# The list loop of route: POOL makes the two products of the high digit's one-hot rows, and DVE compares the high digit first in a chunk

## The chip, the cores and the metric

The kernel runs on one core of one Trainium2 chip. The metric is the device time of one execution in microseconds, median over runs. It is one program of many phases, with a barrier of all engines between them.

## The reference, cut to what matters

The whole is a small vision network: patches are projected to rows of 192, a retention layer follows, then a mixture of experts (16 experts, each picks its 1030 best rows out of 8240 by score), an attention layer, a second mixture (8 experts, two for each row). The change lies in the routing of the first mixture:

```python
scores = jax.nn.sigmoid(x @ gate_weight.T)
topk_score, topk_ids = jax.lax.top_k(scores.T, capacity)      # 16 experts, capacity 1030 of 8240 rows
xg = x[topk_ids]
...
y = jnp.zeros((n, d), x.dtype).at[topk_ids.reshape(-1)].add(out.reshape(-1, d))
shared = jax.nn.silu(hidden_states @ Ws_g.T) * (hidden_states @ Ws_u.T) @ Ws_d.T
return y + shared
```

The order of the chosen rows within an expert's list does not matter to the result.

## The kernel before, in words

`phase_route` finds each expert's threshold by a search over the bits of the score, numbers the chosen rows, and turns these numbers into lists of row indices. The shared expert (`shared_up`, `shared_silu`, `shared_mult`, `shared_rows`, `shared_down`) is computed beside both, ten steps in the search and ten in the list loop.

The list loop has NC = 10 chunks of T = 103 rows (on partitions). In a chunk there are 128 columns (8 images by 16 experts). A chosen row has a place in its expert's list, split into a low digit (0 to 63, plus 1 so that 0 means not chosen) and a high digit (0 to 16). For each column the loop makes a one-hot row of the low digit (64 wide, `hot_lo`, bf16) and two scaled one-hot rows of the high digit (17 wide each, `hot_hi`): the first holds the number of the row's tile, the second the row's number within the tile. One small matmul a column, `hot_hi` transposed by `hot_lo`, adds tile and row number into the right place of the list in PSUM: 128 matmuls a chunk (L785). They are called the list matmuls here.

A chunk on each engine, before:

- PE (TensorE): `shared_up` (three slices of two times two float32 matmuls, L715), `shared_down` (12 matmuls, L725), then it waits for `hot_ready` and does the 128 list matmuls, which end with `hot_used`.
- ACT (ScalarE): the silu of each slice (L800).
- DVE (VectorE): `list_chunk`. It waits for `hot_used` of the chunk before the last (`hot_lo` and `hot_hi` have two halves), then four compares of the low digit (32 columns each, L928), with the three products of the shared expert (L825, which read PSUM) between them; then the compare of the high digit into `hit` (L933), the product of `hit` with `tile0` (L937) and with `row` (L939), which releases PE; the addition of 1 to `tile0` (L942), and the two additions of `shared_rows` (L834), which wait for `shared_down`.
- POOL (GpSimd): memsets at the start of the phase, then 20 DMAs of the scores to DRAM (L705), for which it waits until `turned_out` is 9, like PE and DVE ahead of the loop; after that only the wait for these DMAs.
- SP: loads `h_in` and stores `y_out` of the shared expert, by `y_ready`.

A shared slice uses one of two pairs of PSUM banks: PE's slice f waits for the shared product f - 1 of DVE, and `shared_down` for all three.

`hot_hi` lies in `wide`, and `hit` has one buffer. The order within an engine is that of the code; between engines semaphores alone count. `zero` is a buffer of zeros that PE uses to open and close the accumulation.

Of the kernel before, what the change touches and what calls it, by code (L numbers as in the profile page):

```python
# [8 lines left out]
BF16 = mybir.dt.bfloat16  # L9
I32 = mybir.dt.int32  # L10
U32 = mybir.dt.uint32
ALU = mybir.AluOpType
# [9 lines left out]
T = 103  # L22
NC = SEQ // T
# [17 lines left out]
LB = 64  # L41
HB2 = -(-CAP // LB)
# [3 lines left out]
def names(ctx, nc):  # L46

    sems = []

    def sb(name, shape, dt=F32):
        return ctx.enter_context(nc.sbuf_tensor(name, shape, dt))

    def sem(name):
        sems.append(nc.alloc_semaphore(name))
        return sems[-1]

    def clear():  # L60
        nc.clear_and_free_semaphores(sems)
        nc.all_engine_barrier()

    ctx.callback(clear)
    return sb, sem
# [538 lines left out]
def phase_route(nc, psum, inp, h1, xg, x1T, y, ids, ident, ident_in, consts, consts_in):  # L604
# [9 lines left out]
    FC = FS0 // 128  # L614
# [3 lines left out]
    with ExitStack() as ctx:  # L618
        sb, sem = names(ctx, nc)
        gate, same, before, consts32, row = (consts[n] for n in ("gate", "same", "before", "consts32", "row"))  # L620
        wg, wu, wd = (consts[n] for n in ("wg", "wu", "wd"))
        gpad = sb("rt_gpad", [DP, DC, B, 128])
        iota_lo = sb("rt_iota_lo", [T, LB], BF16)
        iota_hi = sb("rt_iota_hi", [T, HB2], BF16)
        tile0 = sb("rt_tile0", [T, 128], BF16)
# [16 lines left out]
        hot_lo = sb("rt_hot_lo", [T, 2, 128, LB], BF16)  # L642
        hit = sb("rt_hit", [T, 128, HB2], BF16)

        hot_hi = wide[0:T, :, :].rearrange("p k n -> p (k n)").bitcast(BF16)[:, 0:2 * 128 * 2 * HB2] \
            .rearrange("p (a n k) -> p a n k", a=2, n=128)
        zero = sb("rt_zero", [128, 512], BF16)
        idp = sb("rt_idp", [128, 512])
        idT = sb("rt_idT", [128, 4, 128])

# [5 lines left out]
        consts_ready = sem("rt_consts_ready")  # L656
# [4 lines left out]
        step = sem("rt_step")  # L661
        sums_full = sem("rt_sums_full")
        turned, turned_out = sem("rt_turned"), sem("rt_turned_out")
        hit_ready, hot_ready, hot_used = sem("rt_hit_ready"), sem("rt_hot_ready"), sem("rt_hot_used")
        ids_open, ids_full, idp_ready = sem("rt_ids_open"), sem("rt_ids_full"), sem("rt_idp_ready")
        idT_full, idT_ready, ids_ready = sem("rt_idT_full"), sem("rt_idT_ready"), sem("rt_ids_ready")
# [28 lines left out]
        @block.gpsimd  # L695
        def _(pool):
            pool.memset(gpad[:], 0.0).then_inc(zeroed, 1)
            pool.memset(ones, 1.0).then_inc(zeroed, 1)
            pool.memset(zero[:], 0.0).then_inc(zeroed, 1)

            pool.wait_ge(turned_out, 9)
            rows = xg.rearrange("(b c p) d -> p c b d", b=B, c=NC)
            for c in range(NC):
                for lanes in LANES:
                    pool.dma_start(rows[lanes, c, :, D:D + E0], scT[lanes, c, :].rearrange("p (b e) -> p b e", b=B)) \  # L705
                        .then_inc(scores_out, 16)
            pool.wait_ge(scores_out, 32 * NC)

        def shared_up(pe, j, slices=range(FC)):
# [20 lines left out]
        @block.tensor  # L730
        def _(pe):
            pe.wait_ge(ident_in, 16)
            pe.wait_ge(consts_in, ROUTE_CONSTS)
            pe.wait_ge(gpad_ready, 1)
            for s, n in enumerate((W4, W4, SEQ - 2 * W4)):
                for b in range(B):
                    for k in range(DC):
                        last = pe.matmul(psum[:, s, 0:n], gpad[:, k, b, :], x1T[:, k, b, s * W4:s * W4 + n],
                                         start=(b == 0 and k == 0), stop=(b == B - 1 and k == 1))
                last.then_inc(logits_full, 1)  # L740
            pe.wait_ge(score_ready, 3)
            with pe.Fori(0, LOOPS) as j:
                def total(s):
                    pe.wait_ge(counted, j * STEPS + (s + 1))

                    pe.wait_ge(keep_ready, j * STEPS + s)
                    pe.matmul(TOTAL, same[:], count[:], start=True, stop=True).then_inc(totalled, 1)
                shared_up(pe, j, (0,))
                total(0)
                shared_up(pe, j, (1,))  # L750
                total(1)
                shared_up(pe, j, (2,))
                shared_down(pe, j, (0,))
                total(2)
                shared_down(pe, j, (1,))

            def sums(n, weights, rhs, bank):
                pe.wait_ge(step, n)
                pe.matmul(psum[:, bank, 0:1], weights[:], rhs, start=True, stop=True).then_inc(sums_full, 1)

            sums(1, same, small[:, 0:1], 6)
            sums(3, before, rank[:, SEQ - 1:SEQ], 7)
            sums(7, before, rank[:, SEQ - 1:SEQ], 5)

            pe.wait_ge(step, 12)
            for n, src in enumerate((hi, lo, score)):
                for s, c0 in enumerate(range(0, NC, 4)):
                    if 3 * n + s >= 3:
                        pe.wait_ge(turned_out, 3 * n + s - 2)
                    for c in range(c0, min(c0 + 4, NC)):  # L770
                        last = pe.transpose(psum[0:T, s, (c - c0) * 128:(c - c0 + 1) * 128],
                                            src[:, c * T:(c + 1) * T], ident[:])
                    last.then_inc(turned, 1)
            pe.matmul(LISTS, zero[:, 0:128], zero[:], start=True, stop=False, skip_group_check=True)
            pe.wait_ge(turned_out, 9)
            with pe.Fori(0, NC // 2) as i:
                for half in range(2):
                    c = i * 2 + half
                    shared_up(pe, c + LOOPS)
                    shared_down(pe, c + LOOPS)  # L780
                    pe.wait_ge(hot_ready, c + 1)
                    for b in range(B):
                        for e in range(E0):
                            q, g = e % 2, e // 2
                            last = pe.matmul(psum[LB * q:LB * q + 2 * HB2, 6, g * LB:(g + 1) * LB],  # L785
                                             hot_hi[:, half, b * E0 + e, :], hot_lo[:, half, b * E0 + e, :],
                                             start=False, stop=False, skip_group_check=True)
                    last.then_inc(hot_used, 1)
            pe.matmul(LISTS, zero[:, 0:128], zero[:], start=False, stop=True, skip_group_check=True).then_inc(ids_full, 1)
            pe.wait_ge(idp_ready, 1)  # L790
            for g in range(4):
                last = pe.transpose(psum[:, 7, g * 128:(g + 1) * 128], idp[:, g * 128:(g + 1) * 128], ident[:])
            last.then_inc(idT_full, 1)
# [45 lines left out]
        def _(dve):  # L839
# [81 lines left out]
            def list_chunk(c, half, first):  # L921

                lo_c = loT[:, bass.ds(c, 1), :].rearrange("p c n -> p (c n)")
                hi_c = hiT[:, bass.ds(c, 1), :].rearrange("p c n -> p (c n)")
                if not first:
                    dve.wait_ge(hot_used, c - 1)
                for f in range(FC + 1):
                    dve.tensor_tensor(hot_lo[:, half, f * 32:(f + 1) * 32, :],  # L928
                                      lo_c[:, f * 32:(f + 1) * 32].unsqueeze(2).to_broadcast([T, 32, LB]),
                                      iota_lo[:].unsqueeze(1).to_broadcast([T, 32, LB]), ALU.is_equal)  # L930
                    if f < FC:
                        shared_mult(dve, c + LOOPS, (f,))
                dve.tensor_tensor(hit[:], hi_c.unsqueeze(2).to_broadcast([T, 128, HB2]),  # L933
                                  iota_hi[:].unsqueeze(1).to_broadcast([T, 128, HB2]), ALU.is_equal).then_inc(hit_ready, 1)
                dve.wait_ge(hit_ready, c * 2 + 1)

                dve.tensor_tensor(hot_hi[:, half, :, 0:HB2], hit[:], tile0[:].unsqueeze(2).to_broadcast([T, 128, HB2]),  # L937
                                  ALU.mult)
                dve.tensor_scalar(hot_hi[:, half, :, HB2:2 * HB2], hit[:], row[:, 0:1], None, ALU.mult) \  # L939
                    .then_inc(hot_ready, 1)  # L940
                dve.wait_ge(hot_ready, c + 1)
                dve.tensor_scalar(tile0[:], tile0[:], 1.0, None, ALU.add).then_inc(hit_ready, 1)  # L942
                shared_rows(dve, c + LOOPS)

            for half in range(2):
                list_chunk(half, half, True)
# [8 lines left out]
            for side in range(2):  # L955
                for odd in range(2):
                    for q in range(2):
# [3 lines left out]
                        first = LB * q + odd  # L961
# [2170 lines left out]
```

## Time and profile before

| | us |
|---|---|
| runs, median (lowest to highest of 3) | 4561.05 (4549.51 to 4570.84) |
| profiled execution, own time | 4569.56 |
| its span | 4567.8 |
| PE busy | 4034.8 (88%) |
| DVE busy | 2484.5 (54%) |
| ACT busy | 1438.0 (31%) |
| POOL busy | 1249.9 (27%) |

The span is cut by the page into 40 slices of 114 us. The list loop, from about 656 to 870 us, is in slices 6 to 8 (counted from 1):

```profile
PE   8899878699999997665999999999959969899996
DVE  1576468622222222876878787877814355444442
POOL 0221010144444443553010001001012110077775
PEclk9999988899999998775999999999975589999998
```

Each digit is a busy share in tenths (9 is 90% or more); PEclk is the clock that TensorE was granted, in tenths of full speed, where 1.0 is 2.4 GHz and 0.5 is 1.2 GHz. DVE has 6, 8 and 6 there, POOL 1, 0 and 1. The chain that the page follows back from the last instruction stays in the last phase and says nothing of this loop, so the views of single stretches are used below.

### The profile page before, as it was taken

To read this page: it belongs to the slowest core of one execution; us is meant where nothing else is said; L and a number is where in the kernel's file an instruction comes from. 1 tells how busy PE (TensorE), PEld (TensorE's weight loads), DVE (VectorE), ACT (ScalarE), POOL (GpSimd) and SP (SyncE) were. 2 spreads that over 40 slices of the span, in tenths; PEclk is the share of its full clock that TensorE was granted. 3 is DMA by queue.
4 is the path that set the end of the run, shared out by engine and by line. 5 is a ranking of instruction groups with operands and counts; after the bars stand their busy time and mean duration, and the time that the engine had idled before them with its cause. 6 is when DMAs were issued, how large, how long until landed. Compare 5 with 4: busy or idle time off the path is not lost. (4 is left out here: it accounts for less than half of the span.)

```text
span 4567.8 us, 74772 instructions
## 1 busy us (share of the span) xinstructions
PE 4034.8 (88%) x23898; PEld 2458.2 (54%) x23898; DVE 2484.5 (54%) x4593; ACT 1438.0 (31%) x2890; POOL 1249.9 (27%) x1415
## 2 busy tenths in 40 slices
PE   8899878699999997665999999999959969899996
PEld 7788555466666665331333333333315646677774
DVE  1576468622222222876878787877814355444442
ACT  0122110011111111341677777777741111111111
POOL 0221010144444443553010001001012110077775
PEclk9999988899999998775999999999975589999998
DMA  6222111322222221345342224223225211267776
GB/s 217 60 67 54 32 38 28 99 61 60 60 60 60 60 60 28 118 132 107 49 62 44 44 48 61 44 44 51 39 62 158 76 37 46 66 163 172 174 172 154
DMA packets 335914, 361.61 MB, mean 79 GB/s; under 512 B 50364, under 2 KB 297107, under 8 KB 334095
## 3 DMA queue, kind: packets, MB, share of 16 engines
q1 hardware_dynamic: 252191, 274.75, 24.4%
q0 software_dynamic: 61312, 63.66, 8.9%
q10 hardware_dynamic: 22256, 20.93, 1.6%
q8 instruction: 122, 2.00, 0.2%
q14 instruction: 33, 0.27, 0.0%
HBM read 247.51 MB, written 117.00 MB: 80 GB/s over the span
## 5 line engine op out<-in xcount | busy, mean ns | idle before, releaser
L2033 DVE TENSOR_REDUCE at_mx<-psum 128x1 f32<-128x998 f32 (+1 forms) x768 | 884.5, 1189 | 247.2 <-PE psum L1858 246.8
L1988 ACT ACTIVATE at_p<-psum 128x512 f32<-128x512 f32 (+3 forms) x1536 | 851.2, 588 | 294.2 <-PE psum L1932 264.3
L1932 PE MATMUL psum<-at_q,at_k 99*128 99x512 bf16 (+3 forms) x1536 | 518.9, 380 | 21.5 <-issue 16.5
L1858 PE MATMUL psum<-at_k,at_q 96*128 96x512 bf16 (+3 forms) x1536 | 472.9, 390 | 69.4 <-POOL at_identb L1815 31.9
L1918 PE MATMUL psum<-at_p,at_v 128*32 128x486 f32 (+3 forms) x3072 | 405.1, 600 | 1.0 <-ACT at_p L1988 0.7
L1932 PEld LDWEIGHTS psum<-at_q,at_k 99*128 99x128 bf16 (+1 forms) x1536 | 155.0, 102 | 423.9 <-ACT at_p L1988 271.7
L1193 ACT ACTIVATE ex_silu<-psum 128x384 f32<-128x384 f32 (+1 forms) x288 | 131.5, 457 | 774.4 <-PE psum L1137 581.7
L1224 DVE TENSOR_TENSOR ex_hT<-ex_silu,psum 128x384 f32<-128x384 f32 (+1 forms) x288 | 147.5, 512 | 417.1 <-ACT ex_silu L1193 230.3
L1830 POOL DMA_DIRECT2D o_rows<-at_o x96 | 48.5, 505 | 1140.3 <-DVE at_mx L2033 967.0
L1159 PE MATMUL psum<-ex_wd,ex_hT 128*128 128x192 f32 (+1 forms) x1728 | 291.5, 327 | 0.0
L1858 PEld LDWEIGHTS psum<-at_k,at_q 96*128 96x128 bf16 (+1 forms) x1536 | 151.9, 105 | 230.6 <-DVE at_mx L2033 64.0
L1159 PEld LDWEIGHTS psum<-ex_wd,ex_hT 128*128 128x128 f32 (+1 forms) x1728 | 264.1, 179 | 15.9 <-issue 3.6
L2794 POOL DMA_INDIRECT h_rows<-mx_ys,mx_to x144 | 229.3, 1592 | 59.4 <-issue 59.4
L2948 DVE TENSOR_TENSOR mx_hT<-mx_silu,psum 128x256 f32<-128x256 f32 x216 | 91.0, 421 | 271.0 <-ACT mx_silu L2905 212.5
L2905 ACT ACTIVATE mx_silu<-psum 128x256 f32<-128x256 f32 x216 | 82.8, 383 | 479.1 <-PE psum L2847 424.0
L1085 POOL DMA_INDIRECT y_rows<-ex_ys,ex_to x144 | 223.4, 1551 | 33.5 <-issue 33.5
L1132 PE MATMUL psum<-ex_xT,ex_wg 128*128 128x384 f32 (+1 forms) x576 | 230.0, 481 | 0.0
L1133 PE MATMUL psum<-ex_xT,ex_wu 128*128 128x384 f32 (+1 forms) x576 | 213.3, 452 | 0.0
L1137 PE MATMUL psum<-ex_xT,ex_wr 64*128 64x384 f32 (+1 forms) x576 | 207.7, 476 | 0.8
L1138 PE MATMUL psum<-ex_xT,ex_wr 64*128 64x384 f32 (+1 forms) x576 | 207.7, 476 | 0.0
L2765 POOL TENSOR_TENSOR mx_pad<-ident 128x1 f32<-128x1 f32 x144 | 66.1, 459 | 353.6 <-DVE mx_idx L2914 301.9
L1050 POOL TENSOR_TENSOR ex_pad<-ident 128x1 f32<-128x1 f32 x127 | 41.5, 327 | 438.0 <-DVE ex_ys L1237 430.9
(361 smaller groups left out, 7030.7 us busy)
## 6 DMA issues: line engine op xcount, KB each, us to landing
mx_wd<-in_e_dT SPq DMA_DIRECT2D x72, 288.0 KB
qk_parts<-hd_parts SPq DMA_DIRECT2D x32, 579.4 KB, 3.8
at_k<-qk_parts SPq DMA_DIRECT2D x144, 128.8 KB, 5.0
at_q<-qk_parts SPq DMA_DIRECT2D x144, 124.8 KB, 4.6
tok_p<-in_x SPq DMA_DIRECT2D x12, 1176.0 KB
mx_wg<-in_e_gT SPq DMA_DIRECT2D x72, 192.0 KB
mx_wu<-in_e_uT SPq DMA_DIRECT2D x72, 192.0 KB
v_rows<-hd_v_out SPq DMA_DIRECT2D x8, 1536.0 KB
```

The source lines that it names most:

```text
L1085: pool.indirect_dma_start(y, bass.IndirectOffsetOnAxis(ap=to[0:n, half, t:t + 1], axis=0), ys[0:n, half, t, :], None, compute_op=ALU.add). ...
L1132: g = pe.matmul(gate, wg[:, half, cols], xT[:, 0, toks], start=first, stop=not first)
L1133: u = pe.matmul(lift, wu[:, half, cols], xT[:, 0, toks], start=first, stop=not first)
L1137: g = pe.matmul(gate, wr[0:64, half, cols], xT[0:64, 1, toks], start=first, stop=not first)
L1138: u = pe.matmul(lift, wr[64:128, half, cols], xT[64:128, 1, toks], start=first, stop=not first)
L1159: mm = pe.matmul(psum[0:n, 4 + p % 2, (t % 2) * D:(t % 2 + 1) * D], hT[:, f, 128 * t:128 * t + n], wd[:, half, f, :], start=(f == 0), stop ...
L1858: mm = pe.matmul(psum[0:ctx_rows[t], 3 + 2 * ((PRO + n) % 2) + k, 0:w], Q[v][0:R6, j * 1024 + 128 * t:j * 1024 + 128 * t + ctx_rows[t]], K ...
L1918: mm = pe.matmul(psum[32 * j:32 * j + HV, 7, 0:w], V[u][0:n, t, j * HV:(j + 1) * HV], P[0:n, c % 2, j, 0:w], start=(t == 0), stop=(t == CT ...
L1932: pe.matmul(psum[0:n, i % RING, 0:w], K[u][:, j, 128 * t:128 * t + n], Q[u][:, j * 1024 + at:j * 1024 + at + w], start=True, stop=True).th ...
L1988: act.activation(P[0:n, c % 2, j, 0:w], psum[0:n, i % RING, 0:w], ACT.Exp).then_inc(exp_ready, 1)
L2033: dve.tensor_reduce(mx[0:ctx_rows[t], j * CT + t:j * CT + t + 1], pair(n)[0:ctx_rows[t], 0:CTX], AX_X, ALU.max).then_inc(s_free, 1)
L2794: pool.indirect_dma_start(y, bass.IndirectOffsetOnAxis(ap=to[:, r, t:t + 1], axis=0), ys[:, r, t, :], None, compute_op=ALU.add).then_inc(a ...
```

## The change

DVE makes `hit` first in a chunk, before the low digits, and signals it. The two products and the addition to `tile0` move to POOL, behind its DMAs of the scores. `hot_ready` comes from POOL now. A new semaphore `lo_ready` comes from DVE's last low compare, and PE waits for both. A new semaphore `tile_ready` counts POOL's additions to `tile0`. Before DVE writes `hit` again it waits for `hot_ready` of the chunk before. POOL waits for `hot_used` of the chunk before the last. Behind the waits for `hot_used`, `tile_ready` and `hot_ready` POOL has an addition of one column of `zero` into a column of a new small buffer `carried`.

```diff
+        carried = sb("rt_carried", [128, 3], BF16)
...
+        lo_ready, tile_ready = sem("rt_lo_ready"), sem("rt_tile_ready")
...
+            def high_digits(c, half, first):
+                if not first:
+                    pool.wait_ge(hot_used, c - 1)
+                    pool.tensor_tensor(carried[:, 0:1], zero[:, 0:1], zero[:, 0:1], ALU.add)
+                if not (first and half == 0):
+                    pool.wait_ge(tile_ready, c)
+                    pool.tensor_tensor(carried[:, 1:2], zero[:, 0:1], zero[:, 0:1], ALU.add)
+                pool.wait_ge(hit_ready, c + 1)
+                pool.tensor_tensor(hot_hi[:, half, :, 0:HB2], hit[:], tile0[:].unsqueeze(2).to_broadcast([T, 128, HB2]),
+                                   ALU.mult)
+                pool.tensor_scalar(hot_hi[:, half, :, HB2:2 * HB2], hit[:], row[:, 0:1], None, ALU.mult) \
+                    .then_inc(hot_ready, 1)
+                pool.wait_ge(hot_ready, c + 1)
+                pool.tensor_tensor(carried[:, 2:3], zero[:, 0:1], zero[:, 0:1], ALU.add)
+                pool.tensor_scalar(tile0[:], tile0[:], 1.0, None, ALU.add).then_inc(tile_ready, 1)
+
+            pool.wait_ge(consts_ready, 1)
+            for half in range(2):
+                high_digits(half, half, True)
+            with pool.Fori(1, NC // 2) as i:
+                for half in range(2):
+                    high_digits(i * 2 + half, half, False)
             pool.wait_ge(scores_out, 32 * NC)
...
                     pe.wait_ge(hot_ready, c + 1)
+                    pe.wait_ge(lo_ready, c + 1)
...
                 if not first:
                     dve.wait_ge(hot_used, c - 1)
+                if not (first and half == 0):
+                    dve.wait_ge(hot_ready, c)
+                dve.tensor_tensor(hit[:], hi_c.unsqueeze(2).to_broadcast([T, 128, HB2]),
+                                  iota_hi[:].unsqueeze(1).to_broadcast([T, 128, HB2]), ALU.is_equal).then_inc(hit_ready, 1)
                 for f in range(FC + 1):
-                    dve.tensor_tensor(hot_lo[:, half, f * 32:(f + 1) * 32, :],
+                    low = dve.tensor_tensor(hot_lo[:, half, f * 32:(f + 1) * 32, :],
...
+                    if f == FC:
+                        low.then_inc(lo_ready, 1)
                     if f < FC:
                         shared_mult(dve, c + LOOPS, (f,))
-                dve.tensor_tensor(hit[:], hi_c.unsqueeze(2).to_broadcast([T, 128, HB2]),
-                                  iota_hi[:].unsqueeze(1).to_broadcast([T, 128, HB2]), ALU.is_equal).then_inc(hit_ready, 1)
-                dve.wait_ge(hit_ready, c * 2 + 1)
-
-                dve.tensor_tensor(hot_hi[:, half, :, 0:HB2], hit[:], tile0[:].unsqueeze(2).to_broadcast([T, 128, HB2]),
-                                  ALU.mult)
-                dve.tensor_scalar(hot_hi[:, half, :, HB2:2 * HB2], hit[:], row[:, 0:1], None, ALU.mult) \
-                    .then_inc(hot_ready, 1)
-                dve.wait_ge(hot_ready, c + 1)
-                dve.tensor_scalar(tile0[:], tile0[:], 1.0, None, ALU.add).then_inc(hit_ready, 1)
                 shared_rows(dve, c + LOOPS)
```

## Rows read from the trace of the kernel before

**Rows 1.** Busy time of each engine by chunk: stretch, its length, busy (instructions), clock, DMA share, GB/s.

```profile
674.10:696.40 22.30, 17.96 (x176) 12.09 (x176) 17.12 (x13) 1.54 (x3) 0.00 (x0) 0.83 0.11 30
...
719.90:743.60 23.70, 19.38 (x176) 13.15 (x176) 17.23 (x13) 1.54 (x3) 0.00 (x0) 0.79 0.10 27
743.60:764.10 20.50, 16.14 (x176) 11.68 (x176) 17.23 (x14) 1.54 (x3) 0.00 (x0) 0.92 0.11 31
```

**Rows 2.** One chunk in order of time: start, length (us), engine, line, operation.

```profile
743.66 3.50 PE L785 MATMUL psum<-rt_hot_lo,rt_wide 103*34 103x64 bf16 x128 [3.51 <-DVE rt_wide L939]
...
747.09 1.65 PE L715 MATMUL psum<-x1T,rt_wg 96*128 x4
...
750.23 0.58 DVE L825 TENSOR_TENSOR sh_hT<-sh_silu,psum 128x412 f32<-128x412 f32 x1 [3.10 <-PE psum L715]
...
754.11 1.55 PE L715 MATMUL psum<-x1T,rt_wu 96*128 x4
...
755.76 0.58 DVE L825 TENSOR_TENSOR sh_hT<-sh_silu,psum 128x412 f32<-128x412 f32 x1
...
756.48 4.14 PE L725 MATMUL psum<-rt_wd,sh_hT 128*103 128x192 f32 x24 [0.83 <-DVE sh_hT L825]
758.47 2.42 DVE L933 TENSOR_TENSOR rt_hit<-rt_hiT,rt_iota_hi 103x2176 bf16<-103x2176 bf16 x1
760.92 2.43 DVE L937 TENSOR_TENSOR rt_wide<-rt_hit,rt_tile 103x2176 bf16<-103x2176 bf16 x1
763.26 0.81 DVE L939 TENSOR_SCALAR rt_wide<-rt_hit,rt_row 103x2176 bf16<-103x2176 bf16 x1
764.13 3.38 PEld L785 LDWEIGHTS psum<-rt_hot_lo,rt_wide 103*34 103x34 bf16 x128 [3.82 <-DVE rt_wide L939]
...
764.38 1.02 DVE L834 TENSOR_TENSOR sh_y_out<-psum,sh_h_in 103x384 f32<-103x384 f32 x2
```

**Rows 3.** In order of time: POOL's issue of the scores, first and last list matmuls.

```profile
656.96 13.68 POOL L705 DMA_DIRECT2D x_rows<-rt_scT  x20 [194.63 <-ACT rt_scT L813]
...
674.11 2.71 PE L785 MATMUL psum<-rt_hot_lo,rt_wide 103*34 103x64 bf16 x128 [3.50 <-DVE rt_wide L939]
...
866.51 3.51 PE L785 MATMUL psum<-rt_hot_lo,rt_wide 103*34 103x64 bf16 x128 [3.50 <-DVE rt_wide L939]
```

**Rows 4.** POOL's groups by form: busy us, mean ns | idle before; last, one in time.

```profile
L1050 POOL TENSOR_TENSOR ex_pad<-ident 128x1 f32<-128x1 f32 x127 | 41.5, 327 | 438.0 <-DVE ex_ys L1237 430.9 <-POOL ex_idx L1060 3.2 <-DMA y_rows<-ex_ys,ex_to 1.4
...
L357 POOL TENSOR_TENSOR ret_xd<-ret_xn,ret_kdec 103x1536 f32<-103x1536 f32 x10 | 27.5, 2746 | 201.8 <-PE psum L452 192.6 <-DVE ret_xn L550 9.3
L1477 POOL TENSOR_TENSOR hd_v_out<-hd_cen,hd_vrstd 128x1728 f32<-128x1728 f32 x8 | 25.0, 3121 | 0.0
...
L2214 POOL COPY x3T<-pr_xT 96x2060 f32 x6 | 11.4, 1896 | 127.3 <-ACT pr_xT L2303 127.3
...
3494.09 3.42 POOL L2207 TENSOR_TENSOR pr_hb<-pr_hin,pr_bias 128x1536 f32<-128x1536 f32 x1
```

**Rows 5.** POOL and DVE at one time, by time; ns min/median/max in the line with /.

```profile
3416.67 4.39 POOL L2207 TENSOR_TENSOR pr_hb<-pr_hin,pr_bias 128x1536 f32<-128x1536 f32 x1 [16.50 <-issue]
L2320 DVE TENSOR_TENSOR pr_on<-pr_op,pr_recip x1: 4441/4441/4441, 3417.7 to 3417.7; 64x1030 f32<-64x1030 f32 x1
...
3439.06 2.35 DVE L2320 TENSOR_TENSOR pr_on<-pr_op,pr_recip 128x1030 f32<-128x1030 f32 x2
3439.21 5.50 POOL L2207 TENSOR_TENSOR pr_hb<-pr_hin,pr_bias 128x1536 f32<-128x1536 f32 x1 [16.61 <-DVE pr_hout L2331]
...
1850.34 1.31 POOL L1459 TENSOR_TENSOR hd_parts<-hd_left,hd_parts 96x512 bf16<-96x512 f32 x2
1850.60 0.34 DVE L1620 TENSOR_TENSOR hd_part_s<-psum,hd_sin 128x192 f32<-128x192 f32 x1
```

**Rows 6.** DVE's low compare, by form over the whole span: busy us, mean ns.

```profile
L928 DVE TENSOR_TENSOR rt_hot_lo<-rt_loT,rt_iota_lo 103x2048 bf16<-103x2048 bf16 x40 | 91.3, 2284 | 6.6 <-ACT rt_scT L813 6.6
```

**Rows 7.** PE in half a microsecond: busy, granted clock, DMA share, GB/s.

```profile
744.00:744.50 0.50, 0.50 (x28) 0.50 0.00 0
```

More of the change, by code:

```diff
@@ L926, in list_chunk @@
                     dve.wait_ge(hot_used, c - 1)
+                if not (first and half == 0):
+                    dve.wait_ge(hot_ready, c)
+                dve.tensor_tensor(hit[:], hi_c.unsqueeze(2).to_broadcast([T, 128, HB2]),
+                                  iota_hi[:].unsqueeze(1).to_broadcast([T, 128, HB2]), ALU.is_equal).then_inc(hit_ready, 1)
                 for f in range(FC + 1):
-                    dve.tensor_tensor(hot_lo[:, half, f * 32:(f + 1) * 32, :],
-                                      lo_c[:, f * 32:(f + 1) * 32].unsqueeze(2).to_broadcast([T, 32, LB]),
-                                      iota_lo[:].unsqueeze(1).to_broadcast([T, 32, LB]), ALU.is_equal)
+                    low = dve.tensor_tensor(hot_lo[:, half, f * 32:(f + 1) * 32, :],
+                                            lo_c[:, f * 32:(f + 1) * 32].unsqueeze(2).to_broadcast([T, 32, LB]),
+                                            iota_lo[:].unsqueeze(1).to_broadcast([T, 32, LB]), ALU.is_equal)
+                    if f == FC:
+                        low.then_inc(lo_ready, 1)
                     if f < FC:
                         shared_mult(dve, c + LOOPS, (f,))
-                dve.tensor_tensor(hit[:], hi_c.unsqueeze(2).to_broadcast([T, 128, HB2]),
-                                  iota_hi[:].unsqueeze(1).to_broadcast([T, 128, HB2]), ALU.is_equal).then_inc(hit_ready, 1)
-                dve.wait_ge(hit_ready, c * 2 + 1)
-                dve.tensor_tensor(hot_hi[:, half, :, 0:HB2], hit[:], tile0[:].unsqueeze(2).to_broadcast([T, 128, HB2]),
-                                  ALU.mult)
-                dve.tensor_scalar(hot_hi[:, half, :, HB2:2 * HB2], hit[:], row[:, 0:1], None, ALU.mult) \
-                    .then_inc(hot_ready, 1)
-                dve.wait_ge(hot_ready, c + 1)
-                dve.tensor_scalar(tile0[:], tile0[:], 1.0, None, ALU.add).then_inc(hit_ready, 1)
                 shared_rows(dve, c + LOOPS)
```

## Prediction

> **What bounds the kernel now.** I read the page, then the busy time per chunk of the list loop, then the order in time of one chunk, then the durations of every form that is moved, then POOL's own rows. The kernel is a row of phases with a barrier between them, so what the list loop gains or loses passes on whole. In it each of ten chunks takes 20.5 to 23.7 us, PE busy 16 to 19 and DVE 17 of them [rows 1]: neither engine is full, the chunk is a chain over both. The reader should follow it in [rows 2]: the 128 list matmuls start at 743.66, shared_up at 747.09, DVE's first shared product (L825) at 750.23; then compares of the low digit (L928) and shared products take turns, the last shared product ends at 756.34, the last compare, the compare of the high digit (L933), and the two products of its rows (L937, L939) follow, and at 764.13 the list matmuls of the next chunk start: 20.47 us. Shared_down ended at 760.62, so PE stood idle 3.51 us for DVE's rows. The first list matmuls start at 674.11 and the last at 866.51, 192.4 us for nine chunks [rows 3]; six of them have 20.5 and the first three 22.3 to 23.7.
>
> **What the change takes away.** L937 (2.43 us), L939 (0.81) and the short L942 leave DVE. Hit is compared first, before the low digits. If nothing else changed, the list matmuls would wait for shared_down alone: 20.47 - 3.51 = 16.96 us. DVE would keep up: after shared_down come the second row addition (0.6 with its start, of 1.02 for both), hit (2.42) and one low compare (2.28), 5.3 us, while PE needs 3.43 + 3.14 = 6.57 us until the first shared product can run [rows 2].
>
> **What POOL takes.** POOL has no such product in this trace. The first, P1, multiplies 2176 elements by an operand repeated along the inner axis. Nearest is L1477: 3.12 us for 1728 elements, repeated along 16, 1.81 ns each; L357 has 1.79. For 2176 that is 3.9 us. Bounds: 2.0 us, POOL's copy at 1.90 us for 2060 elements; 4.9 us, L2207 with two full operands, 3.42 for 1536 [rows 4]. I take 3.9. The second, P2, has one tensor and one number per partition; nearest is the copy, 0.92 ns each, 2.0 us; above stands a two-operand price, 3.9. I take 2.0. Together S = 5.9 us, with both ends 4.0 to 8.8. The three one-column additions that carry waits cost some 0.3 us each, by the one-column row, and the addition to tile0 hardly more [rows 4]. They come after the products, where DVE makes its last compare beside shared_down; I count them as nothing. If that cover is gone they cost up to 1.2 us a chunk.
>
> The page "GPSIMD Engine Reference" of the Trainium skill, section "Elementwise — side-by-side cycle accounting", gives 4497 ns for a tensor_tensor of 2048 float32; as an estimate that is 4.8 us for P1, and the sum below would be 9 us higher. This trace's repeated-operand rows are quicker than that, and I go by them.
>
> **Whether POOL and DVE can run at once.** This decides the sign. At 3416.67 POOL starts L2207 just after DVE started its first L2320, and DVE's second L2320, normally 1.21 us, lasts 4.44. At 3439.21 POOL starts it 0.15 us behind two of DVE's, 2.35 us in all, and POOL's lasts 5.50 instead of 3.42, 2.08 more: almost all that was left of DVE's [rows 5]. So a DVE instruction with two tensors in SBUF and a POOL instruction that reads SBUF go one after the other in these rows, whole instructions at a time. The shared products read one tensor from PSUM and are not of this kind: L1620, with one operand in PSUM, took 0.34 us from 1850.60 on, inside POOL's two L1459 of 1850.34 to 1851.65, and those were not long for it [rows 5].
>
> The Trainium skill says it as a rule ("SBUF — State Buffer", section "Who interferes with whom"): "A DVE instruction with two SBUF inputs contends with a GpSimd instruction that reads SBUF". By it every compare of this loop stands against every product of POOL. That trace agrees for float32 streams; no row here has bf16 operands with repeated elements, as these compares have.
>
> All five compares of a chunk have two tensors in SBUF, 2.42 + 4 x 2.28 = 11.5 us [rows 6]. I walk through a chunk from the end of shared_down: second row addition 0.6, hit 2.42 (it waits also for POOL's rows of the chunk before, long there), first low compare 2.28 (DVE has it ready when POOL only hears of hit). P1 gets its turn: 3.9. The first shared product lies under it (PE is ready at 6.57). Second compare 2.28; P2 2.0 with the second shared product beneath it; third compare 2.28; third shared product 0.58; shared_down 4.14 [rows 2] with the last compare beneath it. Sum: 0.6 + 2.42 + 2.28 + 3.9 + 2.28 + 2.0 + 2.28 + 0.58 + 4.14 = 20.5 us. The 3.5 us that left the end of the chunk come back as 5.9 of POOL's, less the 2.4 that lie beside PE's matmuls and the first two shared products. Who goes first moves this little, since the pieces add up in any order.
>
> **TensorE's clock.** Before, PE idles 3.5 us ahead of the list matmuls, and the granted clock is 0.50 (1.2 of 2.4 GHz) behind that idle [rows 7]. A mean of 0.92 over a chunk of 20.5 us makes 3.3 us at half clock, 0.83 over 22.3 makes 7.6, 0.79 over 23.7 makes 10 [rows 1]. After, the list matmuls follow shared_down at once. But the idle goes elsewhere: shared_up ends 12.0 us behind the start of the list matmuls (755.66 against 743.66 in [rows 2]), the third shared product, by the walk above, at 16.3. So shared_down starts after an idle longer than the 3.5 us after which the clock fell. At half clock for 3.3 us it gets 1.7 us longer: K = 1.7 a chunk. Bounds: nothing, if the clock stays; 4.1, if all of shared_down runs at half. Gains of the list matmuls at full clock are under DVE's chain and give nothing.
>
> **The start.** POOL issues its 20 DMAs until 656.96 + 13.68 = 670.64 [rows 3], and the new products stand behind them on POOL. DVE's compares of chunk 0 are done by about 669. The first list matmuls can start at 670.6 + 5.9 = 676.6, 2.5 us later than now. The DMAs themselves don't move.
>
> **The sum.** 2.5 + 9 x (20.5 + 1.7) - 192.4 = +9.9 us. In general the difference is 10 x S + 9 x K - 64.4; with S at its ends it is -9 and +39. The profiled execution before took 4569.56 us (span 4567.8); by this it would be 4579. The median of the runs is 4561, 8 us lower, so I give 4571. A measurement of this kernel tells about 0.5% (23 us) from no change.
>
> **The rivals.**
> - *They do run side by side.* The compares with repeated bf16 operands don't hold POOL up, unlike [rows 5]. Then a chunk is 16.96 us, POOL's 5.9 lie beneath DVE's low compares: 2.5 + 9 x 16.96 - 192.4 = -37 us, 4524; down to 4517 if the list matmuls keep full clock (2.7 instead of 3.4 us each). For it: PE's 3.5 us idle is plain. Against: L2320 is slowed in both meetings. Chance 0.15.
> - *POOL's tensor_scalar costs like two operands.* P2 3.9 us, in the middle of DVE's chain of compares: S = 7.8, 78 + 15.3 - 64.4 = +29 us, 4590. It decides from S = 7.2 on (+23). For it: no row has this operation on POOL, and bf16 at that. Against: the copy's 0.92 ns. Chance 0.25.
> - *The clock falls and stays.* K = 4.1, S = 5.9: +32 us, 4593. For it: three chunks before had 7.6 to 10 us at half clock. Against: six had 3.3. Chance 0.07.
> - The forecast, exclusive turns with S near 5.9 and K from 0 to 2.5: -5 to +22 us, 4556 to 4583. Chance 0.53.
>
> Faster than 0.5% is the first rival, 0.15; slower is the second and third, 0.32; between them 0.53. The range goes from 4520 (the first rival nearly whole) to 4600 (the two slow ones, and S at its upper end).
>
> **What would show it.** In the changed trace: P1 near 3.9 us alone, but longer on the record where it waits for a compare; low compares of 4 to 6 us on the record instead of 2.28, above all the second and third; list matmuls right behind shared_down; PE's idle of about 4.3 us before shared_down, and the clock at 0.50 in it; first list matmuls near 676.6; chunks of 22 us. Compares that stay at 2.28 us with chunks of 17 would make the forecast wrong, and so would a P1 or P2 far from 3.9 and 2.0.

## The result, and the profile after

The changed kernel takes 4609.98 us (median of 5 runs, 4606.18 to 4613.22) against 4561.05: ratio 1.0108, interval 1.009 to 1.0125, so 49 us slower. The profiled execution took 4609.77 us with a span of 4608.0, 40 us over the span before. I gave 4571 with a range of 4520 to 4600: too low, the time is outside.

The page after, first its span and busy times, then the slices that answer to those shown of before:

```profile
span 4608.0 us, 74823 instructions
...
PE 4034.3 (88%) x23896; PEld 2460.8 (53%) x23898; DVE 2521.2 (55%) x4563; ACT 1439.5 (31%) x2890; POOL 1425.6 (31%) x1472
...
DVE  1576468723222222785887778878824354444442
...
POOL 0222037634444443465001000100112110067775
```

DVE gave away 34 us of products and is busy 37 us more. That is the first sign: its instructions got longer, not fewer. One chunk in order of time (start, length, engine, line), to be laid beside [rows 2]:

```profile
730.33 2.42 DVE L955 TENSOR_TENSOR rt_hit<-rt_hiT,rt_iota_hi 103x2176 bf16<-103x2176 bf16 x1
732.66 2.29 DVE L958 TENSOR_TENSOR rt_hot_lo<-rt_loT,rt_iota_lo 103x2048 bf16<-103x2048 bf16 x1
732.82 5.84 POOL L718 TENSOR_TENSOR rt_wide<-rt_hit,rt_tile 103x2176 bf16<-103x2176 bf16 x1 [6.65 <-DVE rt_hit L955]
734.86 0.58 DVE L851 TENSOR_TENSOR sh_hT<-sh_silu,psum 128x412 f32<-128x412 f32 x1
735.36 5.44 DVE L958 TENSOR_TENSOR rt_hot_lo<-rt_loT,rt_iota_lo 103x2048 bf16<-103x2048 bf16 x1
738.64 7.85 POOL L720 TENSOR_SCALAR rt_wide<-rt_hit,rt_row 103x2176 bf16<-103x2176 bf16 x1
740.73 0.57 DVE L851 TENSOR_TENSOR sh_hT<-sh_silu,psum 128x412 f32<-128x412 f32 x1
741.22 7.18 DVE L958 TENSOR_TENSOR rt_hot_lo<-rt_loT,rt_iota_lo 103x2048 bf16<-103x2048 bf16 x1
...
748.82 2.28 DVE L958 TENSOR_TENSOR rt_hot_lo<-rt_loT,rt_iota_lo 103x2048 bf16<-103x2048 bf16 x1
...
749.03 6.98 PE L750 MATMUL psum<-rt_wd,sh_hT 128*103 128x192 f32 x24 [8.75 <-DVE sh_hT L851]
...
756.63 2.43 DVE L955 TENSOR_TENSOR rt_hit<-rt_hiT,rt_iota_hi 103x2176 bf16<-103x2176 bf16 x1
```

Read the ends. The first product was issued at 732.82, but the low compare runs until 734.95 and the product ends 3.7 us after that. The second low compare, issued at 735.36, ends 2.1 us behind the product; the second product ends 5.7 us behind that compare; the third compare ends some 1.9 us behind the second product. Each length on the record is its own work plus the wait for the other engine. The shared product at 740.73, which reads PSUM, stays at 0.57. Shared_down starts after 8.75 us of idle and takes 6.98 us instead of 4.14. A chunk is 26.3 us long here, 25.1 in the one before it.

The first and last list matmuls, which answer to [rows 3]:

```profile
678.13 3.60 PE L811 MATMUL psum<-rt_hot_lo,rt_wide 103*34 103x64 bf16 x128 [7.25 <-POOL rt_wide L720]
...
909.61 2.04 PE L811 MATMUL psum<-rt_hot_lo,rt_wide 103*34 103x64 bf16 x128
```

Nine chunks take 231.5 us against 192.4: 25.7 on the mean against 21.4 [rows 1], 39.1 us more. The first list matmuls start 4.0 us later, although the loop began 2.3 us earlier in this execution, so 6.4 us more go before them; the last ones are 1.5 us shorter. In all the list loop is 44 us longer. The spans differ by 40 and the medians by 49, since the profiled execution of the kernel before was itself 8.5 us above its median.

### The profile page after: what moved, and what is told of

Same layout as the page of the kernel before. It is cut to its first block and busy times, and to the rows that moved or that the text cites. A ratio compares the mean times of both kernels' runs of the same rounds, so it can differ in the third digit from the quotient of the medians.

```text
span 4608.0 us, 74823 instructions
## 1 busy us (share of the span) xinstructions
PE 4034.3 (88%) x23896; PEld 2460.8 (53%) x23898; DVE 2521.2 (55%) x4563; ACT 1439.5 (31%) x2890; POOL 1425.6 (31%) x1472
## 5 line engine op out<-in xcount | busy, mean ns | idle before, releaser
L750 PE MATMUL psum<-rt_wd,sh_hT 128*103 128x192 f32 x480 | 107.3, 389 | 86.5 <-DVE sh_hT L851 86.5
```

## The experiments

All times are medians, set beside runs of the kernel before on the same chip; each ratio is to these. The changed kernel itself was not run again beside them, so a difference to it compares two ratios. The times of one kernel scatter by 10 us and more, and the kept traces give a closer measure, the length of the list loop alone: from the start of its first shared_up (L715 before, L740 after) to the first matmul behind the loop (L792 before, L818 after).

| trace | list loop, us | against before |
|---|---|---|
| before | 214.1 | |
| after | 258.1 | +44.0 |
| e1, second product as tensor_tensor | 238.1 | +24.0 |
| e4, iota rows in PSUM | 170.5 | -43.6 |
| e11, the same without POOL | 214.2 | +0.1 |
| e5, the order alone | 207.5 | -6.6 |
| e7, PE filled | 241.9 | +27.8 |
| e8, second product on DVE | 220.3 | +6.2 |
| e9, e4 and e1 together | 169.0 | -45.1 |
| e10, score DMAs behind | 158.3 | -55.8 |

**The second product as a tensor_tensor (e1).**

```diff
-                pool.tensor_scalar(hot_hi[:, half, :, HB2:2 * HB2], hit[:], row[:, 0:1], None, ALU.mult) \
-                    .then_inc(hot_ready, 1)
+                pool.tensor_tensor(hot_hi[:, half, :, HB2:2 * HB2], hit[:], row[:].unsqueeze(2).to_broadcast([T, 128, HB2]),
+                                   ALU.mult).then_inc(hot_ready, 1)
```

> The second product on POOL as a tensor_tensor with row repeated along the inner axis, in place of a tensor_scalar with one number per partition. Theory (POOL and DVE take turns, and the tensor_scalar is dear by its kind of operation): the second product takes 3.9 us undisturbed instead of 5.84, S goes from 9.7 to 7.8, and the kernel is 10 x 1.9 = 19 us faster than the changed one, near 4591. Rival (POOL's price comes from the bf16 data and the 34-wide rows that it writes, whatever the operation): it stays near 5.8 us, and the time near 4610.

4589.12 us, ratio 1.0057 (1.0043 to 1.0072). 49 us of loss became 26, so 23 us came from one product alone, 19 expected; by the loops of the traces it is 20.0. The same arithmetic on the same data is cheaper with two tensors than with one tensor and a number.

**POOL's forms alone (e2).** The changed kernel, with these added where POOL waits during the threshold search; each is waited for before the next. The list loop waits for all of them, but they are done by 532 us, long before it.

```diff
+            for _ in range(3):
+                alone(pool.tensor_scalar(wide16, narrow, row[:, 0:1], None, ALU.mult))
+                alone(pool.tensor_scalar(wide16, narrow, 3.0, None, ALU.mult))
+                alone(pool.tensor_copy(wide16, narrow))
+                alone(pool.tensor_tensor(wide16, narrow, tile0[:].unsqueeze(2).to_broadcast([T, 128, HB2]), ALU.mult))
+                alone(pool.tensor_tensor(wide16, narrow, row[:].unsqueeze(2).to_broadcast([T, 128, HB2]), ALU.mult))
+                alone(pool.tensor_scalar(w32, n32, row[:, 0:1], None, ALU.mult))
+                alone(pool.tensor_copy(w32, n32))
```

> Seven forms on POOL, three times each, in the 190 us in which it waits during the threshold search: on 103x2176 bf16 tensor_scalar with a number per partition, tensor_scalar with a constant, copy, tensor_tensor with tile0 (bf16) and with row (float32) repeated; on 103x256 float32 tensor_scalar and copy. Theory (the operation sets the price): both tensor_scalar near 5.8 us, copy near 2.0, both tensor_tensor near 3.9. Rival 1 (the number per partition is what costs): with the constant 2 to 4 us. Rival 2 (bf16 is what costs): copy near 5 us too, and the float32 tensor_scalar has the copy's price. The time of the whole stays near 4610.

POOL in order of time, the first of the three rounds:

```profile
462.41 5.91 POOL L715 TENSOR_SCALAR rt_hot_lo<-rt_hit,rt_row 103x2176 bf16<-103x2176 bf16 x1
468.41 5.81 POOL L716 TENSOR_SCALAR rt_hot_lo<-rt_hit 103x2176 bf16<-103x2176 bf16 x1
474.29 2.11 POOL L717 COPY rt_hot_lo<-rt_hit 103x2176 bf16<-103x2176 bf16 x1
476.49 3.85 POOL L718 TENSOR_TENSOR rt_hot_lo<-rt_hit,rt_tile 103x2176 bf16<-103x2176 bf16 x1
480.42 3.82 POOL L719 TENSOR_TENSOR rt_hot_lo<-rt_hit,rt_row 103x2176 bf16<-103x2176 bf16 x1
484.34 0.92 POOL L720 TENSOR_SCALAR rt_idp<-rt_idp,rt_row 103x256 f32<-103x256 f32 x1
485.32 0.40 POOL L721 COPY rt_idp<-rt_idp 103x256 f32<-103x256 f32 x1
```

A constant costs what a number per partition costs, the copy of the same bf16 pattern 2.1 us: both rivals fall. It is the operation: 2.7 ns an element as tensor_scalar, 1.8 as tensor_tensor, 1.0 as copy. The copy was no neighbour of the tensor_scalar.

The one run took 4634.56 us, not the 4610 that I expected. Its search takes 152.6 us from the first to the last tried bit against 133.0 in the trace of the changed kernel, and its list loop is as long as there: added work on an idle engine cost some 20 us. The other 5 us of the one run are within the scatter. DVE's instructions on a single element in the search, before, and then in the stretch in which POOL was at work (ns min/median/max):

```profile
L858 DVE TENSOR_TENSOR rt_cand<-rt_th,rt_bit x30: 148/159/160, 493.7 to 626.7; 128x1 int32<-128x1 int32 x30
```
```profile
L903 DVE TENSOR_TENSOR rt_cand<-rt_th,rt_bit x6: 160/2676/4919, 489.8 to 531.2; 128x1 int32<-128x1 int32 x6
...
L903 DVE TENSOR_TENSOR rt_cand<-rt_th,rt_bit x23: 149/159/160, 541.6 to 642.4; 128x1 int32<-128x1 int32 x23
```

One element, two tensors in SBUF, and it waits up to 4.9 us for POOL. The 1285 ns instruction between them (one tensor in SBUF) kept its length, and so did the tensor_scalars on one element (0.14 us).

**The iota rows in PSUM (e4).**

```diff
+            dve.tensor_copy(psum[0:T, 7, 0:LB + HB2], consts32[:, 0:LB + HB2]).then_inc(keep_ready, 1)
+            dve.wait_ge(keep_ready, BITS + 3)
...
-                                  iota_hi[:].unsqueeze(1).to_broadcast([T, 128, HB2]), ALU.is_equal).then_inc(hit_ready, 1)
+                                  psum[0:T, 7, LB:LB + HB2].unsqueeze(1).to_broadcast([T, 128, HB2]), ALU.is_equal).then_inc(hit_ready, 1)
...
-                                            iota_lo[:].unsqueeze(1).to_broadcast([T, 32, LB]), ALU.is_equal)
+                                            psum[0:T, 7, 0:LB].unsqueeze(1).to_broadcast([T, 32, LB]), ALU.is_equal)
```

> The two iota rows lie in an unused PSUM bank, so that DVE's five compares of a chunk read one tensor from SBUF and one from PSUM; all else is the changed kernel, POOL's 9.7 us of products too. Theory (two SBUF inputs make DVE and POOL take turns): compares stay near 2.3 us, POOL's products at 3.9 and 5.84 lie beneath them, a chunk takes some 17 us instead of 25.7, and the kernel is 37 us faster than before the change, near 4525. Rival (semaphores and the order of the handover cost the time, not the SBUF inputs): compares of 5 and 7 us stay, and the time is near 4610.

4523.7 us, ratio 0.991 (0.9889 to 0.9931). A stretch of its list loop in order of time:

```profile
731.21 2.28 DVE L960 TENSOR_TENSOR rt_hot_lo<-rt_loT,psum 103x2048 bf16<-103x2048 f32 x1
731.38 3.85 POOL L718 TENSOR_TENSOR rt_wide<-rt_hit,rt_tile 103x2176 bf16<-103x2176 bf16 x1 [4.81 <-DVE rt_hit L957]
...
734.00 2.28 DVE L960 TENSOR_TENSOR rt_hot_lo<-rt_loT,psum 103x2048 bf16<-103x2048 f32 x1
...
735.21 5.82 POOL L720 TENSOR_SCALAR rt_wide<-rt_hit,rt_row 103x2176 bf16<-103x2176 bf16 x1
...
739.75 4.14 PE L750 MATMUL psum<-rt_wd,sh_hT 128*103 128x192 f32 x24 [0.83 <-DVE sh_hT L851]
...
743.82 2.04 PE L811 MATMUL psum<-rt_hot_lo,rt_wide 103*34 103x64 bf16 x128
```

Side by side, each at its own price. All semaphores, the order and POOL's 9.7 us are those of the changed kernel; one operand moved, and 86 us went. The moved operand is also float32 now and not bf16, but that is not what parts the two engines: the L2320 of [rows 5], which was held up, is float32 too. Chunks are 15.5 us, not 17: the list matmuls no longer follow an idle and take 2.04 us, not 3.5. That the time met the 4525 I expected is partly luck: the chunks are shorter than I said, and the first list matmuls start 6.4 us later in the loop than before, not 2.5.

**PSUM rows without POOL (e11).** The same three edits on the kernel before.

> The kernel before the change with nothing altered but the place of the iota rows (PSUM, not SBUF). Theory (PSUM rows help only by letting POOL read SBUF beside DVE's compares): compares stay at 2.28 and 2.42 us, chunks at 20.5, the time near 4561. Rival (the compares get cheaper by themselves with an operand in PSUM, and the gain of the run with PSUM rows came from that): some 5 us or more faster, with shorter compares.

4560.21 us, ratio 0.9997 (0.9985 to 1.0009). The compares keep 2279 and 2414 ns. So an operand in PSUM gives nothing by itself; it makes room for POOL.

**The order alone (e5).** The kernel before, with the high digit's compare, both products and the addition to `tile0` ahead of the low digits on DVE:

```diff
+                dve.tensor_scalar(tile0[:], tile0[:], 1.0, None, ALU.add).then_inc(hit_ready, 1)
+                for f in range(FC + 1):
+                    low = dve.tensor_tensor(hot_lo[:, half, f * 32:(f + 1) * 32, :],
...
+                    if f == FC:
+                        low.then_inc(lo_ready, 1)
+                    if f < FC:
+                        shared_mult(dve, c + LOOPS, (f,))
-                dve.tensor_scalar(tile0[:], tile0[:], 1.0, None, ALU.add).then_inc(hit_ready, 1)
...
+                    pe.wait_ge(lo_ready, c + 1)
```

> Only the order of the change, nothing on POOL: DVE compares the high digit first and makes both products at once, then the low digits; list matmuls wait for both. Theory (the order is the good half of the change, POOL the bad one): from the end of shared_down 0.6 + 2.42 + 2.43 + 0.81 + 0.2 + 2.28 = 8.7 us until the first shared product instead of PE's 6.6, so a chunk of 16.96 + 2.2 = 19.1 us against 21.4 on the mean before, 20 us faster than before, near 4541. Rival (the order gives nothing, DVE's work only moves from one end to the other): near 4561.

4556.26 us, ratio 0.9983 (0.9969 to 0.9996): 8 us faster by the ratio, not 20. Chunks are 20.4 us. PE in one of them:

```profile
746.93 1.65 PE L716 MATMUL psum<-x1T,rt_wg 96*128 x4 [1.25 <-DVE sh_hT L827]
...
752.40 5.82 PE L726 MATMUL psum<-rt_wd,sh_hT 128*103 128x192 f32 x24 [2.43 <-DVE sh_hT L827]
...
758.15 2.04 PE L787 MATMUL psum<-rt_hot_lo,rt_wide 103*34 103x64 bf16 x128
```

Idles of 1.25 and 2.43 us, then shared_down at 5.82 us. I had left this term out of that expectation; 19.1 + 1.7 is 20.8.

**PE kept at work in the idle (e7).**

```diff
                     shared_up(pe, c + LOOPS)
+                    for _ in range(28):
+                        pe.matmul(psum[:, 7, :], zero[:, 0:128], zero[:], start=True, stop=True)
                     shared_down(pe, c + LOOPS)
```

> The changed kernel with 28 matmuls of zeros (bf16, 128 x 512) into an unused PSUM bank between shared_up and shared_down of every chunk of the list loop, so that PE idles some 2 us there instead of 7.5 to 8.7. Theory (the idle that moved ahead of shared_down costs 1.8 to 2.9 us a chunk through the granted clock, K): shared_down goes from 5.9 and 7.0 us back to 4.1 to 4.3, and the kernel is some 20 us faster than the changed one, near 4590. Rival (the chain is DVE's and POOL's turns alone, the clock costs nothing): near 4610, or above by what the matmuls of zeros delay.

4591.13 us, ratio 1.0061 (1.0047 to 1.0075), some 21 us faster than the changed kernel. Two neighbours of its shared_downs:

```profile
769.15 4.14 PE L750 MATMUL psum<-rt_wd,sh_hT 128*103 128x192 f32 x24 [2.59 <-DVE sh_hT L853]
...
792.50 5.67 PE L750 MATMUL psum<-rt_wd,sh_hT 128*103 128x192 f32 x24 [2.70 <-DVE sh_hT L853]
```

Six of the nine after chunk 0 are at 4.14, three at 5.6 to 5.7.

**The second product back on DVE (e8).**

```diff
+                dve.wait_ge(hit_ready, c + 1)
+                dve.tensor_scalar(hot_hi[:, half, :, HB2:2 * HB2], hit[:], row[:, 0:1], None, ALU.mult)
...
-                pool.tensor_scalar(hot_hi[:, half, :, HB2:2 * HB2], hit[:], row[:, 0:1], None, ALU.mult) \
```

> As the changed kernel, but the second product stays on DVE (0.81 us, right behind hit), POOL makes the first alone (3.9) and the addition to tile0. Theory (POOL's price enters one to one): a chunk from the end of shared_down is 14.6 + 0.85 + 3.9 = 19.3 us, and K of 0 to 1.7 on it: 9 x 19.3 to 21.0 with a start 0.6 us later, so 18 us faster than before to 3 us faster, 4543 to 4558. Rival (each handover to POOL costs by itself, whatever it does): near 4590 or more.

4571.52 us, ratio 1.0017 (1.0008 to 1.0027): 7 us slower than before where at least 3 us faster was expected, a miss by 10 us or more. Its chunks are 21.6 and 22.8 us in turn. One in order of time:

```profile
761.71 4.51 DVE L956 TENSOR_SCALAR rt_wide<-rt_hit,rt_row 103x2176 bf16<-103x2176 bf16 x1
761.75 3.85 POOL L718 TENSOR_TENSOR rt_wide<-rt_hit,rt_tile 103x2176 bf16<-103x2176 bf16 x1 [12.09 <-DVE rt_hit L953]
...
774.41 7.11 PE L748 MATMUL psum<-rt_wd,sh_hT 128*103 128x192 f32 x24 [0.84 <-DVE sh_hT L849]
```

DVE's product, one tensor in SBUF, took 4.51 us instead of 0.81. It ends 0.6 us behind POOL's product, so it waited for POOL too: this kind of DVE instruction (bf16, 0.37 ns an element alone) takes part in the turns. That does not lengthen the sum of 19.3, since DVE would have waited at the next compare. Two other things do. POOL's product now comes ahead of all low compares, so that no shared product of DVE lies beneath it: without K the chunk is 19.8 us by the rows. And shared_down takes 5.82 and 7.1 us: K is 1.7 and 3.0, not 0 to 1.7. Together that is 21.5 and 22.8, and the rival, a price of the handover, isn't needed.

**PSUM rows and two operands (e9); the score DMAs behind (e10).** e9 has the edits of e4 and e1. e10 adds:

```diff
             for half in range(2):
                 high_digits(half, half, True)
+                send_scores(range(half * NC // 2, (half + 1) * NC // 2))
```

and issues no score DMA ahead of the loop.

> The run with the iota rows in PSUM, and the second product on POOL as a tensor_tensor with row repeated. With DVE and POOL side by side POOL's prices are hidden but in chunk 0, where POOL starts behind its 20 DMAs: 2.0 us faster than that run, near 4522. If POOL's products still count in every chunk, it would be 19 us faster, near 4505.

> As the run with PSUM rows and two operands, and POOL issues half of the 20 score DMAs behind the products of chunk 0 and half behind those of chunk 1, not all ahead of the loop. Theory (the queue of DMAs on POOL delays the first list matmuls, PE idle 5 to 7 us): the first list matmuls start when shared_down ends, 5 us earlier, and nothing else moves, near 4517. Rival (the DMAs then collide with a later chunk, or their end delays the phase): near 4522 or above.

e9: 4517.18 us, ratio 0.99 (0.9885 to 0.9915). e10: 4511.69 us, ratio 0.988 (0.9865 to 0.9895), the quickest of all and faster than both kernels. That e9 beats e4 by its 2 us, and e10 beats e9, is within the intervals and not shown by the times; the traces show it where it should be. The loop of e9 is 1.4 us shorter than that of e4, near the 2.0 of the one product in chunk 0 and far from the 19 of the rival. That of e10 is 10.8 us shorter again, twice the 5 expected: the first list matmuls start earlier, and the chunk behind them takes 15.5 us instead of 19.9, as its list matmuls no longer run behind an idle (2.04 us against 3.60). The first list matmuls start at 677.59 in e4, 675.04 in e9, and here in e10:

```profile
656.95 3.85 POOL L720 TENSOR_TENSOR rt_wide<-rt_hit,rt_tile 103x2176 bf16<-103x2176 bf16 x1 [199.59 <-DVE rt_hit L960]
...
665.42 6.96 POOL L709 DMA_DIRECT2D x_rows<-rt_scT  x10
...
669.05 2.04 PE L814 MATMUL psum<-rt_hot_lo,rt_wide 103*34 103x64 bf16 x128
```

## Why the prediction was wrong

**The step that failed is the price of the second product.** It is a term of S, POOL's two products in a chunk. I took "nearest is the copy, 0.92 ns each, 2.0 us" and as upper end "a two-operand price, 3.9". It costs 5.84 us undisturbed (e2, and e4's row), above both ends. So S is 9.7 and not 5.9, and my range for S, 4.0 to 8.8, did not hold it. With S = 9.7 and my own K = 1.7 the formula gives 97 + 15.3 - 64.4 = +48 us; +49 was measured. So close a meeting is partly luck: with the measured K of 2.3 it is +53, and 8 us of overlaps in the chunks (below) and the 1.5 us of shorter last list matmuls bring it down to the 44 by which the loop grew. Of what was missing the one price is 10 x 3.8 = 38 us. My rival on this product had the right place and the right sign, but only 3.9 us and a chance of 0.25. I bounded a missing operation by the neighbours in the trace as if fewer operands had to be cheaper.

**The first product** was 3.9 forecast, 3.85 measured: the row with the same pattern of repetition (L1477) was a good neighbour, and the estimate of 4.8 us from the figure of the Trainium skill's page "GPSIMD Engine Reference" ("Elementwise — side-by-side cycle accounting") would have been 0.9 us too high.

**The turns of DVE and POOL** were right, and e4 against e11 shows them: the compares with bf16 and repeated operands take part like the float32 ones of [rows 5]. The rule of the Trainium skill's page "SBUF — State Buffer" ("Who interferes with whom") holds here, also for one element, as e2 shows. The rival "they do run side by side" is false for this change. Its price was -37 us, and where e4 makes it true the median is 38 us less than before, by the luck told there.

**The sum of a chunk** is a little high. 14.6 (the sum of 20.5 less its S) + 9.7 + K of 2.3 is 26.6, measured 25.7. Most instructions in the chain add some 0.1 us less to it than their own length, as the first low compare at 732.66 starts before the end of hit at 732.75; the third low compare adds 1.9 us instead of 2.28.

**The clock.** My K, what the low clock adds to shared_down, was 1.7. Shared_down took 5.8 to 5.9 and 6.9 to 7.1 us in turn, so K is some 1.7 and 2.8, 2.3 on the mean and 20.8 us in nine chunks. PE at the granted clock in that chunk (stretch, length, PE busy, clock, DMA share, GB/s):

```profile
743.00:744.00 1.00, 0.00 (x0) 1.00 0.00 0
744.00:745.00 1.00, 0.00 (x0) 0.79 0.00 0
745.00:746.00 1.00, 0.00 (x0) 0.50 0.00 0
...
753.00:754.00 1.00, 1.00 (x5) 0.50 0.00 0
754.00:755.00 1.00, 1.00 (x5) 0.59 0.00 0
```

The clock fell in the idle and stayed at half far into shared_down. e7 shortens the idle from 8.7 to some 2.6 us. Its nine shared_downs take 41.8 us instead of 58.0, and its nine chunks are shorter by the same 16.2 us; the medians say 21, which the scatter allows. So most of K is gone there, not all.

The low clock is no new cost of the change, though. Before, it lay on the list matmuls, 3.5 us instead of the 2.04 of e4, and these were on the chain: DVE's first shared product waits 3.10 us for the shared_up behind them [rows 2]. At full clock a chunk before would be 20.47 - 1.46 = 19.0 us and nine of them 171 instead of 192.4. By this estimate the low clock cost about 21 us before and 21 after, in another place, and the loss comes from the turns: 23.4 us a chunk without K, against 19.0.

**The start** was forecast at 676.6 and is 678.13, with a loop that began 2.3 us earlier: so 3.9 us later in the loop than I said, about what the second product lacked (5.84 against 2.0).

**The waits carried by POOL's small additions** cost next to nothing, as forecast; they take up to 2.2 us on the record (they wait for a compare), beside shared_down. Only in the second chunk, where POOL came late, do they stand ahead of the first product, for 0.6 us.

## What to carry to other kernels

Before work moves from DVE to POOL, see which of DVE's instructions beside it read two tensors from SBUF, or are of the quick bf16 kind with one, as in e8: these and POOL add up instead of overlapping. If one operand can lie in PSUM, they overlap, and what was a loss of 49 us is a gain of 38 us (e4), or of 52 with the second product as a tensor_tensor and the score DMAs behind (e10). And don't price an operation that the trace lacks by another that looks simpler: where no row has it, the range must be open above.

## What the runs showed of the hardware that was not expected

- On POOL a tensor_scalar on 103x2176 bf16 takes 5.8 us, with a constant or a number per partition, a tensor_tensor with a repeated operand 3.85, a copy 2.1. In float32 on 256 elements: 0.92 against 0.40.
- DVE's single-element tensor_tensor took up to 4.9 us instead of 0.16 while POOL worked, so work on an idle POOL can slow a chain of tiny DVE instructions (e2, one run, about 20 us for 70 us of POOL's work).
- An idle of 2.4 to 2.7 us ahead of shared_down was enough for a shared_down of 5.6 to 5.8 us in e5 and in three chunks of e7, and not in the others of e7. In e8 a shared_down of 7.1 us follows only 0.84 us of idle: the granted clock had fallen to 0.50 some 4 us before it, behind an idle of 2.49 us ahead of the last slice of shared_up. What decides when the clock falls stays open.
